# Attention and mixture-of-experts in one kernel: the local maxima's transfer moved two slots ahead and before the keys', the last output projection in two parts, other counts of unread products

## The chip, the cores and the metric

The kernel runs on one core of one Trainium2 chip, as one program. The metric is the device time in microseconds (us) of one execution; lower is better. TensorE is called PE here, VectorE DVE, ScalarE ACT, GpSimd POOL and SyncE SP, as the profile does.

## The reference, cut to what matters

```python
x = L0_attn_x                                   # (16, 512, 256) float32: 8192 tokens of 256
x = x + _layernorm(_L0_attn_ref(_layernorm(x), ...))
x = x + _layernorm(_L0_ffn_ref(_layernorm(x), ...))
...
def _L0_attn_ref(x, ...):
    local_out  = _sliding_window_attn(x @ proj_local,  Wl_in, bl_in, Wl_out, bl_out, 128)
    global_out = _sliding_window_attn(x @ proj_global, Wg_in, bg_in, Wg_out, bg_out, 256)
    w = softmax(fusion_w)
    fused = w[0] * local_out + w[1] * global_out
    return layernorm(fused) * ln_gamma + ln_beta
...
    # in each window, 16 heads of 16:
    scores = q @ k.T / 4 + triu(ones(window, window), k=1)
    o = (softmax(scores) @ v) @ W_out.T + b_out
...
def _L0_ffn_ref(x, w_router, w_gate, w_up, w_down):    # 32 experts, capacity 320
    probs = softmax(xt @ w_router); top1 = argmax(probs); gate = probs[top1]
    slot = top1 * C + position of the token among those of its expert, if that is < C
    y = (silu(buf @ w_gate) * (buf @ w_up)) @ w_down     # per expert, on the slots
    return xt + y[slot] * gate
```

## The kernel before

The 8192 tokens are 32 windows of 256. The attention part is a pipeline of 36 steps, 0 to 35, all written out. In step s five windows are in work: a = s (normalise, transpose, project to queries and keys), b = s - 1 (row scores, from which the row maxima come, and the values' projection), c = s - 2 (scores, exponentials, probabilities times values), d = s - 3 (output projection and layer norms, up to x1, the attention's output with its input added), f = s - 4 (norm before the router, logits, the slot of each token, scatter of the rows to DRAM). Each step has 24 slots, k = 0 to 23. Every engine has its own list, in order; the dictionaries `PE_AT`, `ACT_AT` and `DVE_AT` say in which slot it does what, and `PE_LATE`, `ACT_LATE`, `DVE_LATE` say it for steps 33, 34 and 35. Engines meet through semaphores only.

The first 8 slots have to do with local heads (two heads each), the other 16 with one global head each. In slot k PE makes `scores(k, c)` first (lines 1424 and 1427 local, 1432 and 1434 global), then what the dictionaries put there, and last `row_scores(k, b)` (L1507 local, L1510 global). ACT makes the exponential of `scores(k)`, DVE the maximum over each row of `row_scores(k)` (L1025). `scores(u)` waits for exponential u - 2, `row_scores(u)` for maximum u - 2: there are two PSUM banks for each.

Queries and keys are split into three bf16 parts (high on ACT L774, middle on ACT L780, low on POOL L550) and spread by DMA over 96 partitions of a tile `stack`: six transfers of 128 KB for the local queries, six for the local keys (`spread_local(0)` and `spread_local(1)`, L404), and for the global ones 24 of 64 KB (L413). The maxima of each row, negated and in three parts, are three further rows of `stack`: DVE splits them (`split_l` for the local ones, slots 8 to 11), PE transposes them (`maxima_T`, L1526), ACT copies the result to `mT` (`maxima_out`, L823), and SP moves it to `stack` (`maxima_in`, L425, 24 KB). `scores(0)` of the next step can't start without the local one (`m_in[0]`) and `row_scores(0)` not without the local queries and keys (`spread`).

SP's list in a step, in order: the global maxima's transfer; the second half of the global spread, 12 transfers; the load of `xw` (input of a later window); the store of an output window; the local queries' six, the local keys' six; the load of `xr` (the input again, to be added on POOL L617 to give x1); the local maxima's transfer; the first half of the global spread, 12 transfers. SP waits at each for its own semaphore, so whatever is behind it waits too.

The bank `TR` is used in turn by the global maxima's transposes, the output projection (`op0`, `op1`: for each half q of the window four products over the chunks n of `OnT`, L1605) and the local maxima's transposes. DVE reads the projection and adds the bias to give `fbuf`, called f (L1227). In steps 34 and 35 no scores are left, and the steps are a chain through the norms of window 31, its logits and its scatter. Then the experts run, 16 pairs (L1646, L1659, L1670, L1675), from the scattered rows.

`keep_warm(n)` (L1486) makes n products of 512 columns into a bank that nobody reads. They stand at starts and ends of parts; nine follow the logits in each of steps 34 and 35.

Of the kernel before, what the change touches and what calls it, by code (L numbers as in the profile page):

```python
# [8 lines left out]
def attention_moe_program(nc, T, x, pT_l, pT_g, winT_l, winT_g, woT_l, woT_g, bqk_l, bqk_g, bv_l, bv_g,  # L9
# [4 lines left out]
    P = 128  # L14
# [44 lines left out]
    def num(w):  # L59
        return w[1] if w[0] is None else w[0] * 2 + w[1]  # L60
# [11 lines left out]
    with ExitStack() as ctx:  # L72
# [209 lines left out]


        TR_USES = [("mT_g", 2, mT_ready[1], 1, 0), ("op", 3, f_ready, 1, 0), ("mT_l", 1, mT_ready[0], 1, 0)]
        PE_AT = {"xnT": 0, "p0": 2, "x2T": 3, "mT_g": 4, "p1": 5, "lg": 5, "op0": 7, "op1": 9, "p2": 11, "cs": 14, "mT_l": 15, "p3": 15, "v0": 17, "v1": 20, "g3": 1, "g0": 5, "g1": 12, "g2": 18}
        ACT_AT = {"xnT": 0, "xn2": 1, "p0": 2, "mT_g": 4, "x2T": 4, "mid0": 5, "p1": 5, "o_norm": 5, "mid1": 9, "gate": 10, "p2": 11, "f1": 14, "mid2": 14, "mT_l": 16, "p3": 15, "mid3": 17, "v0": 17, "z": 22, "v1": 20, "norm0": 18}
        DVE_AT = {"split_g": 0, "p0": 3, "fold_g1": 4, "p1": 7, "top": 7, "f": 9, "split_l": 8, "p2": 12, "route": 14, "fold_l0": 10, "p3": 16, "fold_l1": 15, "stats_x": 16, "stats_y": 17, "fold_g0": 22, "stats_x1": 23, "moments_x1": 0, "u3": 1, "u0": 6, "u1": 13, "u2": 18}

        LATE = NW + 1
        PE_LATE = (PE_AT, {**PE_AT, "g3": 1, "x2T": 2, "op0": 3, "op1": 4, "lg": 5, "cs": 14}, {**PE_AT, "g3": 1, "x2T": 2, "op0": 3, "op1": 4, "lg": 5, "cs": 14})  # L290
        ACT_LATE = ({**ACT_AT, "z": 19}, {**ACT_AT, "xn2": 1, "x2T": 2, "o_norm": 3, "f1": 14, "gate": 16, "z": 22}, {**ACT_AT, "xn2": 1, "x2T": 2, "o_norm": 18, "f1": 14, "gate": 16, "z": 22})
        DVE_LATE = ({**DVE_AT, "stats_y": 16, "x1": 21, "stats_x1": 23}, {**DVE_AT, "moments_x1": 0, "u3": 1, "fold_g1": 4, "f": 6, "top": 9, "stats_y": 14, "route": 16, "x1": 21, "stats_x1": 22}, {**DVE_AT, "moments_x1": 0, "u3": 1, "fold_g1": 4, "f": 6, "top": 9, "stats_y": 14, "route": 16, "x1": 21, "stats_x1": 22})

# [85 lines left out]
        def _(sp):  # L379
# [48 lines left out]
            def step(s, par):  # L428
                a, b, c, d, f = stages(s)
                ahead = back(s, -2)  # L430
                if c:
                    maxima_in(1, c, par)
                if b:

                    if d:
                        wait_alone(sp, s2_full, nth(d, UNITS, UNITS - 1))
                    spread_global(0, 1, b, 1 - par)
                    spread_global(1, 1, b, 1 - par)
                if a and (ahead[0] is not None or ahead[1] < NW):

                    wait_alone(sp, xn_ready, nth(a, 1))
                    sp.dma_start(xw[:, par, :, :], x_w[bass.ds(num(ahead), 1)].rearrange("w p q f -> (w p) q f")
                                 ).then_inc(x_in[par], 16)
                if f and num(s) < NW + 3:
                    rows_out(f)
                if a:

                    if c:
                        wait_alone(sp, s2_full, nth(c, UNITS, LU - 1))
                    spread_local(0, a, par)  # L450
                    spread_local(1, a, par)
                if d:

                    if exists(back(d, 2)):
                        wait_alone(sp, x1_ready, nth(back(d, 2), 1))
                    sp.dma_start(xr[:, 1 - par, :, :], x_w[bass.ds(num(d), 1)].rearrange("w p q f -> (w p) q f")
                                 ).then_inc(xr_in[1 - par], 16)
                if b:
                    maxima_in(0, b, 1 - par)
                if a:  # L460

                    if c:
                        wait_alone(sp, s2_full, nth(c, UNITS, UNITS - 9))
                    spread_global(0, 0, a, par)
                    spread_global(1, 0, a, par)
                if s[0] is None and s[1] == NW:
                    for e in range(3):
                        expert_weights(e)
# [913 lines left out]
        def _(pe):  # L1382
# [146 lines left out]
            def step(s, par):  # L1529
# [14 lines left out]
                for k in range(UNITS):  # L1544
# [21 lines left out]
                    if f and k == at["lg"]:  # L1566
                        wait_read(pe, PJ_USES, "lg", s, 2)
                        wait(pe, x2T_ready, f)
                        rows = xn2T[:, :, :].rearrange("p n (q j i) -> p n j q i", q=2, i=32)
                        for n in range(2):  # L1570
                            for j in range(4):
                                last = pe.matmul(pj_bank("lg")[32 * j:32 * j + 32, 0:2 * 32].rearrange("e (q i) -> e q i", q=2), wr[:, n, :], rows[:, n, j, :, :],
                                                 start=(n == 0), stop=(n == 1))
                        last.then_inc(lg_full, 1)
                        if num(s) >= NW + 2:
                            keep_warm(9)
                    if a and k == at["p0"]:
                        wait(pe, xnT_ready, a)
                    for j in range(4):
# [6 lines left out]
                    if f and k == at["cs"]:  # L1586

                        wait_read(pe, PJ_USES, "cs", s, 2)
                        wait(pe, hot_ready, f)
                        bank = pj_bank("cs")  # L1590
                        pe.matmul(bank[:, 0:E], earlier[:, :], hot[:, 0, :], start=True, stop=True)
                        pe.matmul(bank[:, E:2 * E], earlier[:, :], hot[:, 1, :], start=True, stop=False)
                        pe.matmul(bank[:, E:2 * E], onesb[:, :], hot[:, 0, :], start=False, stop=True)
                        pe.matmul(bank[:, 2 * E:3 * E], onesb[:, :], hot[:, 0, :], start=True, stop=False)
                        pe.matmul(bank[:, 2 * E:3 * E], onesb[:, :], hot[:, 1, :], start=False, stop=True).then_inc(cs_full, 1)
                    for q in range(2):
                        if d and k == at[f"op{q}"]:
                            if q == 0:
                                wait_read(pe, TR_USES, "op", s, 1)
                                if s[0] is None and s[1] == 3:  # L1600
                                    pe.wait_ge(const_dve, 2)
                                wait(pe, onT_ready[0], d, 2, 1)
                                wait(pe, onT_ready[1], d, 2, 1)
                            for n in range(4):
                                last = pe.matmul(TR[:, q * D:(q + 1) * D], OnT[:, n // 2, n % 2, q * P:(q + 1) * P], wo[:, n, :],  # L1605
                                                 start=(n == 0), stop=(n == 3))
                            if q == 1:
                                last.then_inc(o_full, 1)
                    if b and k == at["mT_l"]:
                        maxima_T(0, b, s)  # L1610
                    for q in range(2):
                        if b and k == at[f"v{q}"]:
                            project_v(q, b, s, 1 - par)
                    if b:
                        row_scores(k, b, 1 - par)

# [126 lines left out]
```

## Time and profile before

| | |
|---|---|
| Median of 3 runs | 1502.93 us (1502.74 to 1506.17) |
| The profiled execution, its own time | 1501.01 us |
| Its span, first to last instruction | 1499.0 us |
| PE busy | 1431.6 us (96%) |
| DVE busy | 1211.0 us (81%) |
| ACT busy | 889.9 us (59%) |
| POOL busy | 725.7 us (48%) |
| Mean granted clock of PE | 0.991 |

A share of busy time doesn't tell what an engine waits for; the views of waits and of the timeline do. In them a number in brackets is the idle time of that engine just before, and what ended it. The clock is given as a share of full speed: 1.00 is 2.4 GHz and 0.50 is 1.2 GHz. The attention part ends at about 1250 us, the experts' part fills the rest.

### The profile page before, as it was taken

Reading aid. Unit: us, or ns where it says so; the run is one execution under the profiler, and the core shown is the slowest. Engines: PE = TensorE matmul, PEld = TensorE weight load, DVE = VectorE, ACT = ScalarE, POOL = GpSimd, SP = SyncE. Lnnn points to the kernel's source line nnn. Section 1 sums busy time; section 2 is a strip of 40 time slices with the busy share of each in tenths; the row PEclk is TensorE's granted clock in tenths of the full one; section 3 lists DMA queues with packets and bytes.
Section 4 is the critical chain, followed back from the end, with each engine's and each line's share of the span. In section 5 each row is a group of like instructions: output and inputs, shape, how many; then the busy total and the mean of one; then the engine's idle time right before and its main releaser. Section 6 shows DMA issues by size and latency. Waiting matters only on the chain. (4 is left out here: it accounts for less than half of the span.)

```text
span 1499.0 us, 38338 instructions
## 1 busy us (share of the span) xinstructions
PE 1431.6 (96%) x13007; PEld 1047.8 (70%) x13007; DVE 1211.0 (81%) x3509; ACT 889.9 (59%) x1907; POOL 725.7 (48%) x1133
## 2 busy tenths in 40 slices
PE   7789999999999999999999999999999888999995
PEld 4567777777777777777777777777777645777773
DVE  6577888888888888888888888888888763888886
ACT  3356767777777777767776777777676632222220
POOL 4114444544554454544545555555554331566665
PEclk9899999999999999999999999999999999999998
DMA  8997566665677777667777766667666313555641
GB/s 147 166 239 194 118 117 113 111 113 115 118 120 115 114 112 112 110 111 112 116 114 116 111 122 112 115 110 116 109 104 102 103 30 119 157 156 166 190 129 39
DMA packets 253411, 183.32 MB, mean 122 GB/s; under 512 B 29446, under 2 KB 251849, under 8 KB 253216
## 3 DMA queue, kind: packets, MB, share of 16 engines
q1 hardware_dynamic: 232976, 165.14, 59.4%
q10 hardware_dynamic: 13328, 12.00, 3.0%
q0 software_dynamic: 6912, 3.73, 1.1%
q8 instruction: 104, 1.70, 0.6%
q14 instruction: 91, 0.75, 0.2%
HBM read 55.78 MB, written 38.04 MB: 63 GB/s over the span
## 5 line engine op out<-in xcount | busy, mean ns | idle before, releaser
L1025 DVE TENSOR_REDUCE mx<-bank 128x2 f32<-128x512 f32 (+1 forms) x768 | 509.7, 672 | 133.9 <-PE bank L1507 107.8
L763 ACT ACTIVATE pt<-bank 128x512 f32<-128x512 f32 x768 | 438.6, 592 | 145.2 <-PE bank L1434 124.2
L1470 PE MATMUL bank<-xnT,weff 128*128 128x256 f32 x1024 | 248.3, 386 | 1.3 <-ACT xnT L855 0.8
L550 POOL TENSOR_TENSOR parts<-rest,parts 128x512 bf16<-128x512 f32 x128 | 149.5, 1168 | 192.3 <-ACT parts L780 192.3
L1470 PEld LDWEIGHTS bank<-xnT,weff 128*128 128x128 f32 x1024 | 187.7, 191 | 26.8 <-ACT xnT L855 1.0
L1510 PE MATMUL bank<-stack 96*128 96x256 bf16 x1024 | 197.5, 274 | 9.0 <-DVE mx L1025 8.6
L1432 PE MATMUL bank<-stack 128*128 128x256 bf16 x1024 | 195.6, 272 | 2.9 <-DMA stack<-mT 1.5
L1510 PEld LDWEIGHTS bank<-stack 96*128 96x128 bf16 x1024 | 83.7, 97 | 95.6 <-DVE mx L1025 46.7
L774 ACT ACTIVATE parts<-bank,bqk 128x256 bf16<-128x256 f32 x256 | 106.9, 469 | 67.8 <-PE bank L1470 66.2
L1646 PE MATMUL bank<-eT,ew 128*128 128x320 f32 x512 | 143.3, 433 | 0.8 <-ACT eT L897 0.8
L1434 PE MATMUL bank<-tri,identb 128*128 128x226 bf16 x512 | 133.2, 260 | 0.0
L1457 PE MATMUL bank<-pt,v_pad 128*32 128x256 f32 x2048 | 123.8, 382 | 0.8 <-ACT pt L763 0.8
L1605 PE MATMUL bank<-wo,OnT 128*128 128x256 f32 x512 | 122.8, 384 | 1.2 <-DVE OnT L1074 1.2
L1646 PEld LDWEIGHTS bank<-eT,ew 128*128 128x128 f32 x512 | 95.9, 190 | 37.7 <-issue 1.4
L1479 PE MATMUL bank<-weff,xnT 128*128 128x512 f32 x256 | 121.2, 596 | 1.1 <-DVE base L1117 1.1
L526 POOL TENSOR_TENSOR ve<-mv,eps 128x2 f32<-128x2 f32 x128 | 25.9, 202 | 185.0 <-DVE mv L946 184.3
L1424 PE MATMUL bank<-stack 128*128 128x128 bf16 x1024 | 100.3, 220 | 14.3 <-DMA stack<-mT 9.3
L1009 DVE SCALAR_TENSOR_TENSOR rest<-bank,bqk,parts 128x256 f32<-128x256 f32 x256 | 108.6, 465 | 6.4 <-ACT parts L774 6.2
L1432 PEld LDWEIGHTS bank<-stack 128*128 128x128 bf16 x1024 | 94.8, 97 | 20.7 <-ACT pt L763 3.6
L906 ACT ACTIVATE sg<-bank 128x320 f32<-128x320 f32 x64 | 28.0, 437 | 132.6 <-PE bank L1646 132.6
L1605 PEld LDWEIGHTS bank<-wo,OnT 128*128 128x128 f32 x512 | 95.1, 192 | 12.3 <-issue 1.4
L556 POOL TENSOR_TENSOR obuf<-obuf,xrow 128x512 f32<-128x512 f32 x32 | 40.5, 1266 | 130.3 <-ACT obuf L813 130.3
(165 smaller groups left out, 2715.7 us busy)
## 6 DMA issues: line engine op xcount, KB each, us to landing
stack<-parts SPq DMA_DIRECT2D x384, 128.0 KB, 4.9
stack<-parts SPq DMA_DIRECT2D x768, 64.0 KB, 2.6
slots_scratch<-zeros ACTq DMA_DIRECT2D x16, 650.0 KB, 6.3
xr<-x SPq DMA_DIRECT2D x32, 256.0 KB
out<-obuf SPq DMA_DIRECT2D x32, 256.0 KB, 3.2
ew<-w_gate SPq DMA_DIRECT2D x32, 256.0 KB, 3.9
ew<-w_up SPq DMA_DIRECT2D x32, 256.0 KB, 4.8
ew<-w_down SPq DMA_DIRECT2D x32, 256.0 KB, 4.2
```

Source lines behind the costliest of these rows:

```text
L550: pool.tensor_tensor(parts[:, j, 2, :], rest[:, j % 2, :], parts[:, j, 1, :], ALU.subtract).then_inc(lo_ready, 1)
L763: act.activation(pt[:, u % PTR, :], S2[u % 2][:, :], ACT.Exp).then_inc(p_ready, 1)
L1009: last = dve.scalar_tensor_tensor(rest[:, j % 2, cols], pj_bank(f"p{j}")[:, cols], bqk[:, b, 2 * qk + t:2 * qk + t + 1], parts[:, j, 0, co ...
L1025: dve.reduce_max(dst, src, AX.X).then_inc(s1_read, 1)
L1432: pe.matmul(bank[:, kb * WIN:(kb + 1) * WIN], k_stack(par, 1, u - LU, kb * P, P), q_stack(par, 1, u - LU, 0, WIN), start=(kb == 0), stop=F ...
L1434: last = pe.matmul(masked, identb[:, :], tri[:, 0:GLO_COLS].unsqueeze(1).to_broadcast([P, 2, GLO_COLS]), start=False, stop=True)
L1457: last = pe.matmul(PV[32 * h4:32 * h4 + 32, half * WIN:(half + 1) * WIN], v_pad[:, par, kb, 1, 8 * (g - 2) + 4 * half + h4, :], pt[:, (u0 ...
L1470: last = pe.matmul(bank[:, t * WIN:(t + 1) * WIN], weff[:, b, c, qk * D + t * P:qk * D + (t + 1) * P], xnT[:, par, c, :], start=(c == 0), ...
L1479: last = pe.matmul(pj_bank(f"v{q}")[:, :], xnT[:, par, c, q * P:(q + 1) * P], weff[:, :, c, 2 * D:3 * D], start=(c == 0), stop=(c == 1))
L1510: last = pe.matmul(bank[:, n * WIN:(n + 1) * WIN], q_stack(par, 1, u - LU, n * P, P, NPART), k_stack(par, 1, u - LU, 0, WIN, NPART), start ...
L1605: last = pe.matmul(TR[:, q * D:(q + 1) * D], OnT[:, n // 2, n % 2, q * P:(q + 1) * P], wo[:, n, :], start=(n == 0), stop=(n == 3))
L1646: last = pe.matmul(banks[2 + 2 * m + n][:, 0:CAP], ew[:, e % 3, n, c, m * P:(m + 1) * P], eT[:, p % 2, c, e % 2 * CAP:(e % 2 + 1) * CAP], ...
```

## The change

Four things change.

- PE transposes the local maxima in slot 13 instead of 15, ACT copies them in slot 14 instead of 16, and SP issues their transfer between the local queries' six transfers and the local keys' six, instead of behind the keys and the load of `xr`.
- In step 34 the output projection is made in two parts: at slot 1, behind the last product with the values, the chunks 0 to 2 of `OnT` for both halves; at slot 3, once chunk 3 is there, the last chunk for both halves. x2T, the transposes for window 30's logits, goes from slot 2 to slot 4 of PE in that step, so behind it.
- Behind the logits of steps 34 and 35 stand seven unread products instead of nine.
- In step 1 one unread product is put into each of slots 2 to 19, ahead of `row_scores`.

```diff
-        PE_AT = {... "cs": 14, "mT_l": 15, "p3": 15, ...}
-        ACT_AT = {... "mid2": 14, "mT_l": 16, "p3": 15, ...}
+        PE_AT = {... "cs": 14, "mT_l": 13, "p3": 15, ...}
+        ACT_AT = {... "mid2": 14, "mT_l": 14, "p3": 15, ...}
...
-        PE_LATE = (PE_AT, {**PE_AT, "g3": 1, "x2T": 2, "op0": 3, "op1": 4, "lg": 5, "cs": 14}, ...
+        PE_LATE = (PE_AT, {**PE_AT, "g3": 1, "x2T": 4, "op0": 3, "op1": 4, "lg": 5, "cs": 14}, ...
...
                     spread_local(0, a, par)
+                if b:
+                    maxima_in(0, b, 1 - par)
+                if a:
                     spread_local(1, a, par)
                 if d:
...
                     sp.dma_start(xr[:, 1 - par, :, :], x_w[bass.ds(num(d), 1)]...
-                if b:
-                    maxima_in(0, b, 1 - par)
...
                         if num(s) >= NW + 2:
-                            keep_warm(9)
+                            keep_warm(7)
...
+                    if d and num(s) == NW + 2 and k == at["g3"]:
+                        wait_read(pe, TR_USES, "op", s, 1)
+                        wait(pe, onT_ready[0], d, 2, 1)
+                        wait(pe, onT_ready[1], d, 2, 0)
+                        for q in range(2):
+                            for n in range(3):
+                                pe.matmul(TR[:, q * D:(q + 1) * D], OnT[:, n // 2, n % 2, q * P:(q + 1) * P], wo[:, n, :],
+                                          start=(q == 0 and n == 0), stop=False)
+                    if d and num(s) == NW + 2 and k == at["op0"]:
+                        wait(pe, onT_ready[1], d, 2, 1)
+                        for q in range(2):
+                            last = pe.matmul(TR[:, q * D:(q + 1) * D], OnT[:, 1, 1, q * P:(q + 1) * P], wo[:, 3, :], start=False, stop=(q == 1))
+                        last.then_inc(o_full, 1)
                     for q in range(2):
-                        if d and k == at[f"op{q}"]:
+                        if d and num(s) < NW + 2 and k == at[f"op{q}"]:
...
+                    if num(s) == 1 and 2 <= k < 20:
+                        keep_warm(1)
                     if b:
                         row_scores(k, b, 1 - par)
```

NW is 32, so NW + 2 is step 34.

## Rows read from the trace of the kernel before

**Rows 1.** PE's waits over the span; then the page's group of line 1605

```profile
PE bank L1424 <- DMA stack<-mT: 9.3, 11, 3.3
...
L1605 PE MATMUL bank<-wo,OnT 128*128 128x256 f32 x512 | 122.8, 384 | 1.2 <-DVE OnT L1074 1.2
```

**Rows 2.** PE's timeline: four step starts (start us, us, engine, line, operation)

```profile
427.12 0.60 PE L1557 MATMUL bank<-ident,xn 128*128 128x128 f32 x4
...
721.22 0.60 PE L1557 MATMUL bank<-ident,xn 128*128 128x128 f32 x4
...
757.06 0.60 PE L1557 MATMUL bank<-ident,xn 128*128 128x128 f32 x4
...
974.07 0.60 PE L1557 MATMUL bank<-ident,xn 128*128 128x128 f32 x4
```

**Rows 3.** PE's timeline at one of the longer steps' ends

```profile
646.86 0.40 PE L1424 MATMUL bank<-stack 128*128 128x128 bf16 x4 [1.48 <-DMA stack<-mT]
```

**Rows 4.** SP's timeline in the step before it

```profile
630.36 7.70 SPq L404 DMA_DIRECT2D stack<-parts  x12
...
638.79 0.77 SPq L425 DMA_DIRECT2D stack<-mT  x1
```

**Rows 5.** Windows there: engines' busy us, PE's clock, DMA share, GB/s

```profile
633.80:643.80 10.00, 10.00 (x79) 5.96 (x78) 9.20 (x30) 7.55 (x16) 6.62 (x12) 1.00 1.17 134
643.80:645.80 2.00, 1.58 (x14) 0.79 (x11) 2.00 (x5) 2.00 (x5) 1.70 (x2) 1.00 1.12 191
```

**Rows 6.** ACT's timeline: `f1` in that step and in the step from 757.06

```profile
633.46 1.08 ACT L793 ACTIVATE fbuf<-fbuf,mr,rstd 128x256 f32<-128x256 f32 x2
...
781.07 1.08 ACT L793 ACTIVATE fbuf<-fbuf,mr,rstd 128x256 f32<-128x256 f32 x2
```

**Rows 7.** SP's timeline in the step from 757.06

```profile
775.94 8.37 SPq L404 DMA_DIRECT2D stack<-parts  x12
```

**Rows 8.** Windows in that step: the last two columns are DMA share and GB/s

```profile
779.10:789.10 10.00, 10.00 (x91) 6.80 (x88) 9.77 (x31) 7.22 (x15) 5.18 (x9) 1.00 1.16 132
789.10:791.10 2.00, 2.00 (x9) 0.93 (x8) 1.57 (x4) 1.91 (x5) 1.44 (x4) 1.00 1.17 194
```

**Rows 9.** Timelines of DVE and PE behind the step end of rows 3

```profile
649.53 0.75 DVE L938 BATCH_NORM_STATS2 bst<-xrow 128x6 f32<-128x256 f32 x2 [3.07 <-POOL xrow L617]
...
653.62 0.63 PE L1551 MATMUL bank<-ident,xn 128*128 128x128 f32 x4 [0.22 <-ACT xn L799]
```

**Rows 10.** Timelines of PE and ACT around the start of step 2

```profile
62.59 0.59 PE L1424 MATMUL bank<-stack 128*128 128x128 bf16 x4 [3.28 <-DMA stack<-mT]
...
66.51 2.55 PE L1470 MATMUL bank<-xnT,weff 128*128 128x256 f32 x8
...
64.50 0.59 ACT L855 ACTIVATE xnT<-bank 128x512 f32<-128x512 f32 x1
```

**Rows 11.** PE's waits in 30 to 60 us; the window behind, with PE's clock

```profile
PE bank L1510 <- DVE mx L1025: 4.6, 8, 1.0
...
61.00:67.80 6.80, 5.21 (x31) 4.62 (x32) 1.57 (x4) 2.28 (x4) 0.00 (x0) 0.50 1.18 147
```

**Rows 12.** PE's timeline in step 34

```profile
1216.42 0.63 PE L1551 MATMUL bank<-ident,xn 128*128 128x128 f32 x4 [0.92 <-DVE xn L1169]
1218.28 5.30 PE L1605 MATMUL bank<-wo,OnT 128*128 128x256 f32 x16 [1.22 <-DVE OnT L1074]
...
1223.87 2.12 PE L1486 MATMUL bank<-tri,identb 128*128 128x512 bf16 x9
```

**Rows 13.** Timelines of POOL and DVE in step 34

```profile
1221.78 1.27 POOL L556 TENSOR_TENSOR obuf<-obuf,xrow 128x512 f32<-128x512 f32 x1 [1.07 <-ACT obuf L813]
...
1223.62 0.69 DVE L1227 TENSOR_TENSOR fbuf<-bank,bias_row 128x512 f32<-128x512 f32 x1 [5.49 <-PE bank L1605]
...
1225.75 0.70 POOL L530 TENSOR_TENSOR rstd<-ve,mhalf 128x2 f32<-128x2 f32 x1
...
1227.88 0.88 DVE L1143 SCALAR_TENSOR_TENSOR ybuf<-ybuf,rstd,beta_row 128x256 f32<-128x256 f32 x2
```

More of the change, by code:

```diff
@@ L284, in attention_moe_program @@
         TR_USES = [("mT_g", 2, mT_ready[1], 1, 0), ("op", 3, f_ready, 1, 0), ("mT_l", 1, mT_ready[0], 1, 0)]
-        PE_AT = {"xnT": 0, "p0": 2, "x2T": 3, "mT_g": 4, "p1": 5, "lg": 5, "op0": 7, "op1": 9, "p2": 11, "cs": 14, "mT_l": 15, "p3": 15, "v0": 17, "v1": 20, "g3": 1, "g0": 5, "g1": 12, "g2": 18}
-        ACT_AT = {"xnT": 0, "xn2": 1, "p0": 2, "mT_g": 4, "x2T": 4, "mid0": 5, "p1": 5, "o_norm": 5, "mid1": 9, "gate": 10, "p2": 11, "f1": 14, "mid2": 14, "mT_l": 16, "p3": 15, "mid3": 17, "v0": 17, "z": 22, "v1": 20, "norm0": 18}
+        PE_AT = {"xnT": 0, "p0": 2, "x2T": 3, "mT_g": 4, "p1": 5, "lg": 5, "op0": 7, "op1": 9, "p2": 11, "cs": 14, "mT_l": 13, "p3": 15, "v0": 17, "v1": 20, "g3": 1, "g0": 5, "g1": 12, "g2": 18}
+        ACT_AT = {"xnT": 0, "xn2": 1, "p0": 2, "mT_g": 4, "x2T": 4, "mid0": 5, "p1": 5, "o_norm": 5, "mid1": 9, "gate": 10, "p2": 11, "f1": 14, "mid2": 14, "mT_l": 14, "p3": 15, "mid3": 17, "v0": 17, "z": 22, "v1": 20, "norm0": 18}
         DVE_AT = {"split_g": 0, "p0": 3, "fold_g1": 4, "p1": 7, "top": 7, "f": 9, "split_l": 8, "p2": 12, "route": 14, "fold_l0": 10, "p3": 16, "fold_l1": 15, "stats_x": 16, "stats_y": 17, "fold_g0": 22, "stats_x1": 23, "moments_x1": 0, "u3": 1, "u0": 6, "u1": 13, "u2": 18}
         LATE = NW + 1
-        PE_LATE = (PE_AT, {**PE_AT, "g3": 1, "x2T": 2, "op0": 3, "op1": 4, "lg": 5, "cs": 14}, {**PE_AT, "g3": 1, "x2T": 2, "op0": 3, "op1": 4, "lg": 5, "cs": 14})
+        PE_LATE = (PE_AT, {**PE_AT, "g3": 1, "x2T": 4, "op0": 3, "op1": 4, "lg": 5, "cs": 14}, {**PE_AT, "g3": 1, "x2T": 2, "op0": 3, "op1": 4, "lg": 5, "cs": 14})
         ACT_LATE = ({**ACT_AT, "z": 19}, {**ACT_AT, "xn2": 1, "x2T": 2, "o_norm": 3, "f1": 14, "gate": 16, "z": 22}, {**ACT_AT, "xn2": 1, "x2T": 2, "o_norm": 18, "f1": 14, "gate": 16, "z": 22})
```

## The prediction

> **What bounds the kernel now.** I read the page first. TensorE (PE) is busy 96% of the span; it sets the pace, so a part of the change is worth what it takes from PE's waits, or from the chain where PE only waits. The table of PE's waits comes next [rows 1]: its longest entry is the transfer of the maxima (`stack<-mT`), 9.3 us in 11 waits. Third, PE's timeline around step starts; I date a step by the transposes of line 1557. An undisturbed stretch of six steps takes 974.07 - 757.06 = 217.01 us, 36.17 each; the eight steps from 427.12 to 721.22 take 294.10 [rows 2]. Against 8 x 36.17 = 289.36 these lose 4.7 us. In [rows 3] the reader sees how: PE has nothing left before `scores(0)`, line 1424, and sits for 1.48 us until the transfer lands. Fourth, SyncE's queue (SP) shows why: the transfer of 24 KB is issued at 638.79 and is there at 646.86, 8 us later, since it stands behind twelve of 128 KB and `xr` [rows 4]. The DMA engines are full meanwhile (share 1.17 and 1.12): 134 GB/s in the middle of it, with 191 in 643.8 to 645.8 [rows 5], says that the twelve (1.57 MB, 11.8 us at 134) are through at about 644.7, and the first six at 638.8.
>
> **The local transfer, two slots sooner and ahead of the keys.** PE's two transposes move from slot 15 to 13: same work. They can't add a wait: `row_scores(13)` in the same slot waits for VectorE's (DVE) maximum(11), and that stands behind the last split on DVE's list. The copy on ScalarE (ACT), counted 0.4 us, moves behind the two activations of `f1`, which end at 634.54 [rows 6]; it pushes exp(15) back by that much, and PE asks for that only two slots on. So mT is ready at about 634.9. SP reaches it at 634.2 at the soonest (630.36 plus half of 7.70 [rows 4]) and waits 0.7; it issues mT (0.77), then the six key transfers from about 635.8 instead of 634.2, then `xr`, then the global ones. So the keys are issued 1.7 us later here. In the regular step that starts at 757.06, `f1` ends at 782.15, mT is ready at 782.5, and the keys are issued in 783.3 to 787.2, where the twelve were done at 784.31: 2.9 us later [rows 6, 7]. Queued behind SP's waiting instruction are: the six keys (for `row_scores(0)` of the next step), `xr` (for x1 on GpSimd, POOL), and twelve global ones, first needed in slot 8 of the next step. What hides the later issue is the queue's backlog: the six query transfers still keep the engines busy until about 638.8, and the keys' first come before that. I take it that the keys land 0.3 to 1 us later only. In the regular step they are there by 791.1, when the stage of 132 to 194 GB/s ends [rows 8], and PE wants them at 757.06 + 36.17 + 0.4 = 793.6; in the step that ends at 646.86 it would want them at 646.4 and has them at 644.7 plus up to 1.
>
> The Trainium skill, "DMA: Bandwidth & Descriptors", section "Rules for kernel authors", speaks against this order: a transfer whose slowest dimension is below 16 keeps to that many DMA engines. The destination of mT has three rows, so its 48 pieces of 512 B would pile on three engines, now ahead of the keys. No row here tells engines apart; by that rule the keys would come at the late end of my range, and the sum would be about 1 us smaller. The numbers below don't need it.
>
> Worth: with mT early, all steps would take 36.17. That is 4.7 us in the eight steps. Of the table's 9.3 us, 3.3 stand at 62.59 [rows 10]; 6.0 - 4.7 = 1.3 are left elsewhere, of which I take 0.6, half: **5.3 us**. But `xr` gives some back. Where it lands late, POOL's x1 is late, then its statistics, and then x2T in slot 3. At 649.53 they start 2.27 us after PE's step start (646.86 + 0.40), and PE waits 0.22 [rows 9]; so each us beyond 2.05 costs one. With the stall of 1.48 gone the step starts about 1.3 sooner, and the wait becomes 1.5. Two weaker cases of the kind I put at half of that together, 0.8: 2.3 us, which lessens the 5.3. **Steady part: 3.0 us**; bounds 0 and 6.0.
>
> **Unread products in step 1, and its end.** 18 products of 512 columns are put in (slots 2 to 19). Nine of line 1486 take 2.12 us at the upper clock [rows 12], 0.213 each between starts: 3.8 us of PE work. Their cover: step 1 has eight waits of 4.6 us for DVE in its global half alone [rows 11], and then the stall of 3.28 us. If the cover were gone, they would cost 3.8. In that stall sits the gain. Without it PE still can't run on: ACT makes exp(0) and xnT only behind its list of weight DMAs, xnT at 64.50 to 65.09, and p0 can't start before 65.15; it started at 66.51 [rows 10]: 1.35. Also p0's eight instructions took 2.55 us, where eight of that shape take 1.9 at 0.24 each [rows 1], in a stretch with the clock granted at 0.50, its lower level of 1.2 GHz, after the stall [rows 10, 11]; with a shorter one I count 0.45 back. **1.8 us**. Bounds: 3.8 lost, or the whole stall, 3.3, gained.
>
> **The last output projection.** In step 34 only the chain counts. PE ends `values` at about 1215.5 (1216.42 less the idle 0.92), waits 1.22 for OnT until 1218.28, and then makes all 16 instructions (8 products of two each) in 5.30 us; DVE's f starts at 1223.62 [rows 12, 13]. Now 12 of 16 run from 1215.5: at 0.24 each (122.8 us for 512 [rows 1]) that is 2.9 us, to 1218.4, and 4 behind the wait take 0.95: f at about 1219.3, 4.3 us sooner. What is late next? POOL: it has the residual until 1223.05 and only then makes rstd for f: 0.3 for two small ones and 0.70, so 1224.1, against 1226.45. DVE's second scaling, at 1227.88, needs it [rows 13]: 1224.2. So **3.7 us**. x2T, moved behind the four products, starts at 1219.3 instead of 1216.42, and its logits come at about 1221.1, when DVE has just finished f's statistics. That move costs nothing while f's chain is the longer; if the logits were the last, they would eat up to 0.5. Two fewer unread products after the logits give at most 2 x 0.213 = 0.4 in each of the last two steps, if DVE's `hot` isn't later; I count 0.1. **Sum 3.8**; bounds 2.9 (the clock stays at the lower level, so four products and x2T take twice as long) and 4.7. The experts' part hides none of it, since it starts on the last scatter.
>
> **Sum.** 3.0 + 1.8 + 3.8 = 8.6 us. The profiled execution took 1501.01 (span 1499.0), so 1492.4 for it. The median of the runs is 1.9 above it, 1502.93: **1494.3 us**.
>
> **Rivals.** (1) *The keys land as late as they are issued*: the queue runs dry between queries and keys. Regular steps: 791.1 + 2.9 = 794.0 against 793.6, 0.4 in each of 22; in the eight others 645.8 + 1.7 = 647.5 against 646.4, 1.1 each: 17.6 of new stalls, for 5.3 of old ones. 1494.3 + 3.0 + 12.3 = 1509.6, slower. For it: in the regular step the twelve end near 790.4, so the first six near 784.5, and the keys' issue now starts at 783.3, little ahead. Against: ahead is ahead, and only a dry queue makes it so. It decides once (8.6 + 4.5) / 30 = 0.4 us are lost per step. Chance 0.07. (2) *Only the eight slow steps stall*: 8 x 1.1 = 8.8 in place of 5.3; 1494.3 + 3.0 + 3.5 = 1500.8, no change. Chance 0.10. (3) *The products in step 1 lie on the path* and the start gains nothing: 1494.3 + 1.8 + 3.8 = 1499.9, no change. Against: the cover above. Chance 0.05. My forecast has 0.78.
>
> **Range.** Highest gain 6.0 + 3.3 + 4.7 = 14.0: 1488.9. Upwards cases (2) and (3) begin at 1499.9; I take 1489 to 1500. A difference under 0.3% (4.5 us) can't be told from no change with this kernel. Faster 0.78, same 0.15, slower 0.07.
>
> **What the profile after would show.** Waits for `stack<-mT` at `scores(0)` gone or one or two; no or few waits of `row_scores` for `stack<-parts`; in SP's list the transfer from mT between two groups of six; x2T waiting 1 to 2 us in some steps with a late `xr`; the clock around 61 to 67.8 less low; in step 34 twelve instructions before and four behind the wait for OnT, f about 4.3 sooner, and the start of the experts about 8.6 sooner. Wrong would make it: keys that wait in every step, or an experts' part that lasts longer.

## The result, and the profile after

The changed kernel takes 1497.87 us (median of 7 runs, 1494.49 to 1500.03) against 1502.93 us (7 runs, 1500.07 to 1506.17) for the kernel before: ratio 0.9962, 95% interval [0.9947, 0.9976]. That is 5.1 us or 0.3% faster: inside the range, 3.6 us above the 1494.3 forecast, and about 0.6 of the 8.6 us that were to be gained.

The profiled execution took 1497.85 us, its span is 1496.0: 3.0 us less than before. (The profile before was 1.9 us faster than the median of its kernel, this one lies on the median.) PE's waits over the span and its busy time on the page (engine, line, what it waited for, us in total, times, longest):

```profile
PE 1433.1 (96%) x13021; PEld 1047.0 (70%) x13021; DVE 1214.9 (81%) x3509; ACT 874.9 (58%) x1907; POOL 722.8 (48%) x1133
...
PE bank L1425 <- ACT pt L764: 7.5, 30, 2.1
...
PE bank L1511 <- DVE mx L1026: 7.0, 12, 2.3
PE bank L1508 <- issue: 5.0, 2, 2.7
PE bank L1552 <- ACT xn L800: 4.7, 7, 1.5
```

The entry `stack<-mT`, 9.3 us [rows 1], is gone. In its place L1508 (`row_scores` of local heads; lines have moved by one) has two waits of 5.0 us in all with no releaser named; by the code it waits there for the local queries and keys or for DVE's maximum, and in step 4 DVE's last maximum had ended 2.4 us before PE went on. So I read them as waits for keys. L1552 (x2T) has 4.7 us in 7. To see where the 3.0 us came from I cut both executions at step starts, PE's transposes of xn. Before:

```profile
29.95 0.38 PE L1557 MATMUL bank<-ident,xn 128*128 128x128 f32 x2
...
173.58 0.38 PE L1557 MATMUL bank<-ident,xn 128*128 128x128 f32 x2
...
1118.97 0.38 PE L1557 MATMUL bank<-ident,xn 128*128 128x128 f32 x2
...
1249.96 0.88 PE L1631 MATMUL bank<-ident,zb 128*128 128x128 f32 x6
```

After, with the wait in step 4 among them, and the experts' start:

```profile
30.84 0.60 PE L1558 MATMUL bank<-ident,xn 128*128 128x128 f32 x4
...
137.34 0.60 PE L1558 MATMUL bank<-ident,xn 128*128 128x128 f32 x4
140.62 0.38 PE L1508 MATMUL bank<-stack 96*128 96x128 bf16 x4 [2.67 <-issue]
...
177.58 0.38 PE L1558 MATMUL bank<-ident,xn 128*128 128x128 f32 x2
...
1119.67 0.38 PE L1558 MATMUL bank<-ident,xn 128*128 128x128 f32 x2
...
1246.98 0.88 PE L1647 MATMUL bank<-ident,zb 128*128 128x128 f32 x6
```

| stretch | before | after | gain |
|---|---|---|---|
| to the start of step 1 | 29.95 | 30.84 | -0.9 |
| steps 1 to 4 | 143.63 | 146.74 | -3.1 |
| steps 5 to 30 | 945.39 | 942.09 | +3.3 |
| step 31 to the experts | 130.99 | 127.31 | +3.7 |
| experts | 249.0 | 249.0 | 0 |

So the middle and the end came as forecast (3.0 and 3.8), and the start went the other way. Three things more are needed for what follows. First, in the middle nothing waits for keys, and x2T waits for ACT 2.1 us in all, as was forecast; PE's waits in 180 to 1120 us:

```profile
PE bank L1425 <- ACT pt L764: 4.0, 25, 0.2
PE bank L1552 <- ACT xn L800: 2.1, 5, 0.7
```

SP's list in a regular step (from 757.69) has the new order; the keys are issued until 788.16, 3.2 us later from the step's start than in [rows 7]:

```profile
777.48 3.83 SPq L404 DMA_DIRECT2D stack<-parts  x6
783.44 0.78 SPq L425 DMA_DIRECT2D stack<-mT  x1
784.32 3.84 SPq L404 DMA_DIRECT2D stack<-parts  x6
788.26 0.55 SPq L459 DMA_DIRECT2D xr<-x  x1
```

Second, step 3. The same part of SP's list, and the windows there (last three columns: PE's clock, DMA share, GB/s):

```profile
123.24 7.15 SPq L404 DMA_DIRECT2D stack<-parts  x6
130.49 0.77 SPq L425 DMA_DIRECT2D stack<-mT  x1
131.39 5.44 SPq L404 DMA_DIRECT2D stack<-parts  x6
```

```profile
128.00:132.00 4.00, 4.00 (x42) 1.91 (x40) 3.51 (x10) 2.94 (x6) 3.21 (x6) 1.00 0.98 241
132.00:136.00 4.00, 4.00 (x28) 2.54 (x24) 3.09 (x9) 2.92 (x6) 2.11 (x7) 1.00 0.49 115
136.00:140.00 4.00, 1.94 (x18) 1.19 (x16) 2.17 (x5) 3.24 (x7) 0.00 (x0) 1.00 1.13 134
140.00:144.00 4.00, 3.38 (x33) 1.69 (x37) 0.83 (x3) 0.60 (x1) 2.17 (x2) 0.64 0.97 158
```

Six query transfers take SP 7.15 us to issue here, not 3.83, and the keys 5.44. SP is done with the keys at 136.83, only 1.1 us before PE wants them (137.34 + 0.6); in the step from 757.69 it is 6.2 us. PE waits 2.67 us, its clock is lower behind the wait (0.64 in the last window), and step 4 lasts 40.24 us (137.34 to 177.58) where a regular one lasts 36.1. From 132 to 136 the DMA engines also work at 0.49 only: the queue runs dry, as in the first rival. Whether that makes the wait, the experiments have to tell.

Third, step 34, against [rows 12, 13]: PE, DVE and POOL:

```profile
1215.98 2.86 PE L1603 MATMUL bank<-wo,OnT 128*128 128x256 f32 x12
1218.74 1.13 PE L1608 MATMUL bank<-wo,OnT 128*128 128x256 f32 x4
1219.91 0.69 DVE L1228 TENSOR_TENSOR fbuf<-bank,bias_row 128x512 f32<-128x512 f32 x1 [1.22 <-PE bank L1608]
1222.34 1.26 POOL L557 TENSOR_TENSOR obuf<-obuf,xrow 128x512 f32<-128x512 f32 x1 [1.07 <-ACT obuf L814]
1222.72 0.91 DVE L1098 CAST idx_f<-top_i 128x2 f32<-128x2 uint32 x1
1223.86 0.70 POOL L531 TENSOR_TENSOR rstd<-ve,mhalf 128x2 f32<-128x2 f32 x1
1224.97 0.88 DVE L1144 SCALAR_TENSOR_TENSOR ybuf<-ybuf,rstd,beta_row 128x256 f32<-128x256 f32 x2
```

Twelve instructions before the wait and four behind it. The products with the values begin 0.55 us later here than before (1214.12 against 1213.57), so f, at 1219.91, is 1223.62 + 0.55 - 1219.91 = 4.3 us sooner, and the second scaling 1227.88 + 0.55 - 1224.97 = 3.5.

Part of these 4.3 us is the clock. The 16 products took 5.30 us before and take 2.86 + 1.13 = 3.99 us now. Before, PE's granted clock was 0.69 over them, of which the lower level from about 1218.1 to 1221.6, behind two waits; now it is 1.00:

```profile
1218.28:1223.58 5.30, 5.30 (x20) 4.16 (x24) 0.00 (x0) 0.91 (x2) 3.47 (x6) 0.69 0.02 3
...
1215.98:1219.91 3.93, 3.93 (x22) 3.22 (x19) 2.48 (x6) 0.00 (x0) 2.46 (x5) 1.00 0.02 4
```

So about 3.0 us come from the twelve instructions moved ahead of the wait, and 1.3 from the spell of the lower clock that stays away.

### The profile page after: what moved, and what is told of

It is laid out like the page before. It is cut to its first block and busy times, and to the rows that moved or that the text cites. A ratio compares the mean times of both kernels' runs of the same rounds, so it can differ in the third digit from the quotient of the medians.

```text
span 1496.0 us, 38366 instructions
## 1 busy us (share of the span) xinstructions
PE 1433.1 (96%) x13021; PEld 1047.0 (70%) x13021; DVE 1214.9 (81%) x3509; ACT 874.9 (58%) x1907; POOL 722.8 (48%) x1133
## 5 line engine op out<-in xcount | busy, mean ns | idle before, releaser
L1511 PEld LDWEIGHTS bank<-stack 96*128 96x128 bf16 x1024 | 85.3, 97 | 94.2 <-issue 47.8
L1662 PE MATMUL bank<-eT,ew 128*128 128x320 f32 x512 | 143.3, 433 | 0.8 <-ACT eT L898 0.8
L1662 PEld LDWEIGHTS bank<-eT,ew 128*128 128x128 f32 x512 | 96.2, 191 | 37.4 <-issue 1.4
L1619 PE MATMUL bank<-wo,OnT 128*128 128x256 f32 x496 | 117.5, 380 | 0.0
L1508 PE MATMUL bank<-stack 96*128 96x128 bf16 x1024 | 100.1, 220 | 5.9 <-issue 5.0
L1508 PEld LDWEIGHTS bank<-stack 96*128 96x128 bf16 x1024 | 73.5, 97 | 40.4 <-issue 19.6
## 6 DMA issues: line engine op xcount, KB each, us to landing
stack<-parts SPq DMA_DIRECT2D x384, 128.0 KB, 4.6
```

Source lines behind the costliest of these rows:

```text
L1508: last = pe.matmul(bank[:, (2 * n + j) * P:(2 * n + j + 1) * P], q_stack(par, 0, 2 * u + n, j * P, P, NPART), k_stack(par, 0, 2 * u + n, j ...
L1511: last = pe.matmul(bank[:, n * WIN:(n + 1) * WIN], q_stack(par, 1, u - LU, n * P, P, NPART), k_stack(par, 1, u - LU, 0, WIN, NPART), start ...
L1662: last = pe.matmul(banks[2 + 2 * m + n][:, 0:CAP], ew[:, e % 3, n, c, m * P:(m + 1) * P], eT[:, p % 2, c, e % 2 * CAP:(e % 2 + 1) * CAP], ...
```

## The experiments

Times are medians; a ratio is to the kernel before on the same chip. The kernel before spread over 14 us in one set of 35 runs (1498.76 to 1513.04) and over 7 and 12 us in the two others, the versions over 4 to 10 us, so I lean on the stretches of the profiles, cut as above. Each is one execution, so differences of a stretch that are smaller than those between two profiles of one kernel show nothing.

| version | steps 1 to 4 | steps 5 to 30 | 31 to experts | ratio, interval |
|---|---|---|---|---|
| before | 143.6 | 945.4 | 131.0 | |
| before, second profile | 150.9 | 948.0 | 131.1 | |
| changed | 146.7 | 942.1 | 127.3 | 0.9962 [0.9947, 0.9976] |
| changed, second profile | 146.0 | 941.4 | 127.6 | |
| transfer alone | 146.7 | 941.9 | 131.0 | 0.9968 [0.9947, 0.9988] |
| products alone | 144.8 | 943.6 | 132.9 | 0.9991 [0.9972, 1.0009] |
| projection alone | 148.0 | 946.7 | 129.3 | 0.9978 [0.9961, 0.9995] |
| changed, SP's list as before | 147.3 | 942.8 | 128.0 | 0.9961 [0.9943, 0.9978] |
| changed, new order from step 4 | 143.3 | 941.6 | 127.8 | 0.9950 [0.9933, 0.9968] |
| changed, `xr` first | 147.0 | 939.2 | 127.5 | 0.9945 [0.9927, 0.9963] |
| both of these | 143.2 | 938.8 | 127.4 | 0.9930 [0.9904, 0.9957] |
| changed, zero fills spread | 143.6 | 943.1 | 127.5 | 0.9955 [0.9937, 0.9973] |
| changed, old slots | 146.8 | 963.2 | 130.8 | 1.0129 [1.0093, 1.0165] |
| changed, x2T in slot 2 | 145.8 | 940.2 | 128.0 | |

### One part at a time

The transfer alone: the slots of PE and ACT and the order on SP, on the kernel before.

```diff
-"mT_l": 15   # PE_AT
+"mT_l": 13
-"mT_l": 16   # ACT_AT
+"mT_l": 14
...
                     spread_local(0, a, par)
+                if b:
+                    maxima_in(0, b, 1 - par)
+                if a:
                     spread_local(1, a, par)
```

> Only the local maxima's transfer is changed: slots 13 and 14, and ahead of the keys in SP's list. Theory A: this part gains about 3.3 us in steps 5 to 30 and loses about 4 us where row_scores(0) of step 4 waits for the keys (a wait of 2 to 3 us at about 140 us, the DMA share low just before it, then a stretch at the half clock). In sum it stands within 1.5 us of before, and step 4 lasts about 40 us. Theory B: the wait in step 4 has to do with the products put into step 1. Then this kernel has no such wait, step 4 lasts 36 us, and it is 3 to 4 us faster than before.

Measured: 1500.03 us against 1504.97. Steps 5 to 30 take 941.9 us; step 4 lasts 40.0 us and has the wait, 2.5 us, without any product in step 1. Theory A holds for the place of the wait. Its price came out smaller against the runs (ratio 0.9968) than against the first profile, for a reason that the next profiles show.

The products alone:

```diff
+                    if num(s) == 1 and 2 <= k < 20:
+                        keep_warm(1)
                     if b:
                         row_scores(k, b, 1 - par)
```

> Only the 18 unread products in step 1. Theory A: they cost nothing that lasts and gain little, since the end of step 1 waits for transfers: within 1 us of before, the stall of some 3 us at scores(0) of step 2 still there, step 4 lasts 36 us. Theory B: step 4 lasts about 40 us here too, and the kernel is 3 to 4 us slower than before.

Measured: 1503.31 us, ratio 0.9991: no difference that can be told. The stall at `scores(0)` of step 2 is still there, 3.35 us. Step 4 lasts 35.8 us, so theory B falls. The last stretch, 132.9 us in the table, holds a spell of the lower clock at 1176 to 1188 us (0.82 and 0.89 in windows of 6 us), which the kernel before doesn't have there.

The projection alone, with nine products behind the logits:

```diff
+                    if d and num(s) == NW + 2 and k == at["g3"]:
+                        ...  # chunks 0 to 2 of both halves
+                    if d and num(s) == NW + 2 and k == at["op0"]:
+                        ...  # chunk 3 of both halves
-"x2T": 2   # PE_LATE, step 34
+"x2T": 4
```

> Only the last output projection in two parts, with x2T moved behind it in step 34; nine unread products stay. The prediction's step: 3.7 us faster, f on DVE 4.3 us sooner after the end of the values' products, y's second scaling 3.7 us sooner. Rival: the scatter of window 30, or the output's rows on POOL, hold the end, and it gains 1 to 2 us.

Measured: 1500.91 us, ratio 0.9978, which is 3.3 us [0.8, 5.9]. Counted from the start of the last products with the values, f comes 4.3 us sooner and the second scaling 3.5, as in the changed kernel. The stretch from step 31 shows 129.3 instead of 131.0, but that profile has a spell of the lower clock level at 1186 us. The eight other profiles with the projection split and the new slots have none there, and in them the stretch takes 127.3 to 128.0: 3.0 to 3.8 us less than 131.0 and 131.1, the two profiles of the kernel before, and than 131.0, the transfer alone, which has the new slots and the old projection.

The changed kernel with SP's list as before:

```diff
                     spread_local(0, a, par)
-                if b:
-                    maxima_in(0, b, 1 - par)
-                if a:
                     spread_local(1, a, par)
...
+                if b:
+                    maxima_in(0, b, 1 - par)
```

> The changed kernel with SP's list as before: PE's and ACT's slots for the local maxima stay at 13 and 14, but the transfer is again issued behind the keys and the load of xr. Theory A (the place in SP's list makes both the gain in the middle and the loss in step 4): step 4 lasts 36 us again, but the stalls at scores(0) in the middle are back (about 4 to 6 us), so within 1 us of the changed kernel. Theory B: step 4 stays at 40 us, and the kernel is 3 us or more slower than the changed one.

Measured: 1499.12 us, ratio 0.9961. Neither theory as written. Step 4 lasts 37.4 us, but step 3 now ends with 3.5 us at `scores(0)`, and steps 1 to 4 take 147.3. In the middle some stalls for the maxima are back:

```profile
PE bank L1424 <- DMA stack<-mT: 2.8, 4, 1.0
PE bank L1424 <- issue: 2.8, 9, 0.8
```

and yet steps 5 to 30 take 942.8, nearly as little as with the new order. So the earlier slots by themselves seem to be worth most of the middle's gain; it is one profile against 943.6 to 948.0 in the four with the old slots and order. Part of it is that an undisturbed step lasts 36.12 instead of 36.17 us; why, no run here tells.

### Is the start steady?

Both kernels once more, unchanged.

> The kernel before, unchanged, for one more profile. If the start of the kernel is steady, steps 1 to 5 take 143.6 us again and the stall at scores(0) of step 2 is 3.3 us. If it varies by itself, they take up to 148 us, as the same stretch did with only the projection changed (147.95).

Measured: 1511.66 us for this execution. Steps 1 to 4 take 150.9 us, 7.2 more than in the first profile of the same program, with a wait of 3.4 us at the end of step 3 that the first had as 0.9. PE's waits in the first 180 us:

```profile
PE bank L1424 <- DMA stack<-mT: 6.4, 2, 3.4
```

So the first profile had caught a good start. Versions with the old order took 143.6, 150.9, 144.8, 148.0 and 147.3 us in steps 1 to 4, 146.9 in the mean; those with the new order in all steps and the fills as before 146.7, 146.0, 146.7, 147.0, 146.8 and 145.8, 146.5 in the mean. The change moves the start by less than the start moves by itself.

> The changed kernel, unchanged, for one more profile. If the wait for the keys in step 4 belongs to the order of the transfers, it is there again, at 2 to 3 us, and step 4 lasts about 40 us; if it was a chance of the one execution, it is gone.

Measured: 1497.15 us; the wait for the keys in step 4 is there, 1.7 us, and step 4 lasts 38.4 us, both less than expected. It is there in all five profiles with the new slots, the new order in every step and the fills as before (the changed kernel twice, the transfer alone, `xr` first, x2T in slot 2), with 1.7 to 2.7 us. It is no chance.

### The wait for the keys in step 4

The new order only from step 4 on:

```diff
-                if b:
+                if b and num(s) >= 4:
                     maxima_in(0, b, 1 - par)
...
+                if b and num(s) < 4:
+                    maxima_in(0, b, 1 - par)
```

> The changed kernel, but in steps 1 to 3 the local maxima's transfer stands behind the keys and the load of xr in SP's list, as before; from step 4 on it stands ahead of the keys. Theory A (in step 3 the queue runs dry between queries and keys, so the keys' landing follows their later issue): the wait of 2.7 us at row_scores(0) at the start of step 4 is gone or under 1 us, step 4 lasts 36 to 37.5 us, steps 5 to 30 take 942 us as in the changed kernel; from step 1 to step 5 it takes about 144 us instead of 146.7. Rival: the start of the kernel varies by some us by itself, in any version, and the wait only takes another name (scores(0) for the maxima): steps 1 to 5 take 146 to 148 us again, and the time is within 1 us of the changed kernel.

Measured: 1497.12 us, ratio 0.9950. Step 4 lasts 35.8 us, no wait for keys, 1.6 us for the maxima in its place, at the end of step 3; steps 1 to 4 take 143.3. These are theory A's numbers, but they don't rule its rival out. Up to the end of step 3 this kernel issues its transfers exactly like the version with SP's list as before, and that one waited 3.5 us there and took 147.3. In the seven profiles with the old order in step 3 the wait for the maxima is 0.9 to 3.5 us, 2.0 in the mean, and steps 3 and 4 together take 72.0 to 76.1, 73.4 in the mean. In the five with the new order the wait for the keys is 2.2 us in the mean and the two steps take 73.0 to 75.5, 74.3 in the mean. So the wait takes another name, as the rival says, and the new order costs the start some 0.8 us, less than it varies by itself.

The zero fills, 16 transfers of 650 KB which ACT issues in steps 2 and 3, spread as 6, 4 and 6 over steps 2 to 4:

```diff
-if s[1] in (2, 3) and k < 16 and k % 2 == 1:
-    zero_slots((s[1] - 2) * 8 + k // 2)
+if s[1] in (2, 3, 4) and k % 2 == 1 and k < (12, 8, 12)[s[1] - 2]:
+    zero_slots((0, 6, 10)[s[1] - 2] + k // 2)
```

> The changed kernel with the 16 zero fills of the slots (650 KB each, from ACT's queue) spread over steps 2 to 4 as 6, 4, 6 instead of 8 and 8 in steps 2 and 3. Theory: SP issues slowly in step 3 (0.9 us for a key transfer instead of 0.64) and the queue runs dry because the fills crowd the DMA engines; with half of them in step 3 the query and key transfers are issued faster and the wait for the keys at row_scores(0) of step 4 goes from 1.8 to 2.7 us to under 1 us. Rival: SP is late for another reason, and the wait stays at 2 us or more; then steps 1 to 5 take 146 us or more.

Measured: 1496.58 us, ratio 0.9955. SP's list in step 3:

```profile
121.95 4.00 SPq L404 DMA_DIRECT2D stack<-parts  x6
128.45 0.77 SPq L425 DMA_DIRECT2D stack<-mT  x1
129.34 4.18 SPq L404 DMA_DIRECT2D stack<-parts  x6
```

The order is the same as in the changed kernel, but six transfers take SP 4.0 and 4.2 us, the keys start 2 us sooner, the wait is gone, and step 4 lasts 36.1 us. In the changed kernel the last fill is issued at 124.8 us, beside the queries; here the last one of step 3 at 115.0. The wait moved in part: step 5, behind the fills of step 4, now lasts 38.0, with 0.90 us at `row_scores(0)` and 0.95 at x2T. So the fills make the keys late.

But a dry queue is not what makes the wait. Either is seen without the other: with the fills spread the DMA share is 0.53 from 128 to 132, and 0.10 in the us from 129, and PE doesn't wait; in the transfer alone it is never below 1.08 from 128 to 138, and PE waits 2.49 us.

```profile
128.00:132.00 4.00, 4.00 (x29) 2.25 (x30) 3.32 (x9) 3.98 (x10) 3.66 (x3) 1.00 0.53 100
```

```profile
132.00:136.00 4.00, 4.00 (x26) 2.47 (x25) 3.35 (x9) 3.45 (x7) 1.72 (x6) 1.00 1.13 154
```

What goes with the wait is how long before PE's demand SP is done with the keys: 1.1 to 3.8 us in the five profiles with the wait, 5.8 with the fills spread, 6.2 in the regular step (and 5.0 in the later one behind the spread fills, with its 0.90 us). How long the keys take to land behind that isn't the same in all: the wait ends 5.2 and 5.9 us after the end of their issue in the transfer alone and in `xr` first, 3.4 to 3.8 us in the other three. So SP's late issue and full DMA engines can both have a part; the runs don't tell them apart.

### How much cover is left in the middle

The old slots 15 and 16 with the new order, so that SP waits longer with the keys behind it:

```diff
-"mT_l": 13   # PE_AT
+"mT_l": 15
-"mT_l": 14   # ACT_AT
+"mT_l": 16
```

> The changed kernel, but PE and ACT make the local maxima's transposes and copy in slots 15 and 16 as before, while SP's list keeps the transfer ahead of the keys. SP then waits some 1.5 us longer, with the keys behind it. Theory (the backlog of the query transfers covers the later issue, up to a point which the changed kernel has nearly reached): the queue now runs dry, the keys land 1 us or more later, and row_scores(0) waits for them in most steps, 0.3 to 1 us each; steps 5 to 30 take 950 to 965 us. Rival: the queue has more cover than that, and they stay at 942.

Measured: 1522.96 us, ratio 1.0129: 19 us slower than before, 24 than the changed kernel by the span. Steps 5 to 30 take 963.2, as the theory said, but by a longer way. SP's list and PE's waits (180 to 1140 us):

```profile
384.21 3.87 SPq L404 DMA_DIRECT2D stack<-parts  x6
391.94 0.77 SPq L425 DMA_DIRECT2D stack<-mT  x1
392.81 3.84 SPq L404 DMA_DIRECT2D stack<-parts  x6
```

```profile
PE bank L1552 <- ACT xn L800: 13.6, 25, 1.3
PE bank L1508 <- issue: 2.9, 6, 0.9
```

SP stands still for 3.9 us (388.08 to 391.94) and then has the keys and `xr` behind it. The keys account for 2.9 us; x2T, late through `xr`, x1 and its statistics, for 13.6, in nearly every step. That is why the most regular steps last 36.62 us here, half a us more.

### The load of xr, and the best version

`xr` at the head of SP's list in each step:

```diff
+                if d:
+                    if exists(back(d, 2)):
+                        wait_alone(sp, x1_ready, nth(back(d, 2), 1))
+                    sp.dma_start(xr[:, 1 - par, :, :], ...)
                 if c:
                     maxima_in(1, c, par)
...
                     spread_local(1, a, par)
-                if d:
-                    ...
```

> The changed kernel with the load of xr moved to the head of SP's list in each step, where the DMA engines are nearly idle. Theory: the waits of x2T for ACT, 2.1 us in 5 between 180 and 1120 us, come from xr landing late, so they go, the keys land about 1 us sooner, and steps 5 to 30 take 939 to 940 us instead of 942.1. Rival: the late statistics have another cause (z on ACT), and the waits stay: 942.

Measured: 1495.65 us, ratio 0.9945. No wait of x2T between 180 and 1120 us is left, steps 5 to 30 take 939.2:

```profile
PE bank L1425 <- ACT pt L764: 2.6, 16, 0.2
PE bank L1425 <- issue: 1.3, 8, 0.2
PE bank L1508 <- issue: 0.7, 1, 0.7
```

Both edits together, the new order from step 4 and `xr` first:

> The changed kernel with both: the load of xr at the head of SP's list, and the local maxima's transfer ahead of the keys only from step 4 on. If the two effects add, steps 1 to 5 take 143 to 145 us, steps 5 to 30 take 939.2, the part from step 31 to the experts 127.5, and it is 4 to 5 us faster than the changed kernel, about 10 us faster than before. Rival: the start varies by itself by as much, so steps 1 to 5 take 146 to 148 here and it is only 2.5 us faster than the changed kernel.

Measured: 1493.72 us, ratio 0.9930 [0.9904, 0.9957]: 10.5 us faster than before by the ratio, 8.7 by the medians. The middle is that of `xr` first, 938.8, which is 26 steps of 36.11. The start, 143.2, is as short as with the new order from step 4 alone, but by what is said there it may owe that to chance. PE's only waits in the middle:

```profile
PE bank L1427 <- ACT pt L766: 3.7, 23, 0.2
```

### The place of x2T in step 34

```diff
-"x2T": 4   # PE_LATE, step 34
+"x2T": 2
```

> The changed kernel with x2T left in slot 2 in step 34, between the two parts of the last projection. The prediction's reading (POOL's rstd, not PE, holds y's second scaling): f comes 0.3 to 0.7 us later than in the changed kernel, but the part from step 31 to the experts stays at 127.3 to 127.8 us. Rival: f's chain is the bound, and the part takes 0.5 us more, 128 or above.

One profile: the stretch takes 128.0 us, the rival's side of the line, against 127.3 and 127.6. Counted from the start of the last products with the values, f comes 0.3 us later and the second scaling 0.5. This profile has a spell of the lower clock from about 1223 us, but the second scaling starts at 1222.63, so its half us is not the clock's. POOL's rstd was ready at 1221.78; DVE's list held the scaling, in which one small instruction had lost 1.0 us (last section). Whether the chain of f or that loss sets the end stays open.

## Why the prediction was right or wrong

**Steady part, forecast 3.0 us: right.** 3.3 in the pair of profiles. The four profiles with the middle as before take 943.6 to 948.0, 945.9 in the mean, the five with the middle of the changed kernel 940.2 to 942.1, 941.4 in the mean: 4.5 us less (the one with the fills spread, whose step 5 waits behind fills, left out). The stalls at `scores(0)` are gone. The give-back by `xr` was forecast as 2.3; x2T waits 2.1 us (0.2 before), and the version with `xr` first, without these waits, gains 2.9 in the middle, which shows that it hangs on `xr`. The keys, forecast 0.3 to 1 us later, make no wait in 26 steps. Not foreseen: the slots alone shorten the undisturbed step by 0.05 us and seem to bring most of the gain; the new order adds about 1 us net of what `xr` costs, by one profile.

**The last projection, 3.8: right.** 3.7 in the pair, f 4.3 us sooner as worked out. The sum took the 16 instructions at the upper clock's 0.24 us without saying that the 5.30 us before held a spell of the lower level; 1.3 of the 4.3 us hang on that spell staying away. The lower bound of 2.9 was for that case. The reading of what comes next was wrong: I had POOL's rstd hold the second scaling. It was ready at 1224.56, but DVE began at 1224.97, since its own list had lost 0.74 us on one instruction (below). So 3.5 instead of 3.7 there; that the two products fewer gave the rest isn't shown.

**The end of step 1 and the products, forecast 1.8: wrong.** Nothing of it is left: steps 1 and 2 take 71.24 us against 71.67 before, 71.61 with the transfer alone and 71.47 with the products alone. The stall at `scores(0)` is gone, but two others stand in its place, and behind them p0 is slow:

```profile
62.23 0.38 PE L1508 MATMUL bank<-stack 96*128 96x128 bf16 x4 [2.33 <-issue]
65.82 0.61 PE L1425 MATMUL bank<-stack 128*128 128x128 bf16 x4 [2.10 <-ACT pt L764]
66.55 3.31 PE L1471 MATMUL bank<-xnT,weff 128*128 128x256 f32 x8
```

Counted from the start of step 1, p0 starts 0.85 us sooner (35.71 instead of 36.56), where 1.35 was forecast; and its eight instructions take 3.31 us, not 2.55, where 0.45 was to come back. The step that failed is that a shorter stall gives the upper clock back: the idle time was only shared out, 4.4 us in two pieces for 3.3 in one, and the keys' wait was not in the sum. The products are neither cost nor gain that can be measured.

**The keys in the start: wrong.** "I take it that the keys land 0.3 to 1 us later only" was drawn from steps 17 and 21 and applied to all. In step 3 SP needs 7.15 us for six transfers where I reckoned 3.85, the fills being in flight, and is done with the keys 1.1 us before PE wants them: 2.67 us of wait and a spell at the lower clock level behind it, 4.1 us in that step. The version with the fills spread has no such wait. The first rival, the dry queue, is seen in that profile, but not in all that wait, so it is not the cause. Against the profile before this looks like a loss of 3.1 us in steps 1 to 4; over all profiles it is some 0.8, since with the old order the start waits for the maxima instead.

**The base, and the sum.** I had made the sum against a profile whose steps 1 to 4 were 1.1 to 7.2 us shorter than in the four others with the old order in every step. A single profile can't tell that; the second one did. It accounts for the ratio of the runs, 5.7 us [3.6, 8.0], being more than the 3.0 of the pair of spans. Over all profiles the three parts are 4.5, -0.8 and 3.0 to 3.8 us, where 3.0, 1.8 and 3.8 were forecast: the middle gave more, for reasons that I hadn't seen, and that made up for about half of what the start lacked. That much of the agreement is luck.

**The rule of the Trainium skill** ("DMA: Bandwidth & Descriptors", "Rules for kernel authors") on transfers with few rows in their slowest dimension: the keys came late enough in no regular step to see it, so these runs neither bear it out nor contradict it.

## What to carry to other kernels

A transfer moved ahead in a queue is paid for by those behind it. Whether they notice has to be looked up in each stage, above all where other transfers run beside them: take the time from the end of their issue to where they are wanted. The DMA share alone misleads. When a stall is taken away, look at what else was just in time: here `xr`, whose early issue was worth nearly as much again (2.9 us) as the change's middle part (3.3). When a chain has idle time in it, read the clock behind it too: 1.3 of the 4.3 us by which f came sooner were the clock's. And profile the kernel before twice before weighing effects of a few us.

## What the runs showed of the hardware that was not expected

- While POOL makes its addition of 128x512 (1222.34 to 1223.60), DVE's cast of 128x2 takes 0.91 us and ends at 1223.63; the same cast takes 0.16 to 0.18 us in the other 31 steps. In the version with x2T in slot 2, DVE's tensor_scalar of 128x2 takes 1.19 us and ends within 0.03 us of the end of the same addition:

```profile
1219.50 1.26 POOL L557 TENSOR_TENSOR obuf<-obuf,xrow 128x512 f32<-128x512 f32 x1 [1.07 <-ACT obuf L814]
...
1219.60 1.19 DVE L1092 TENSOR_SCALAR ntop<-top 128x2 f32<-128x2 f32 x1
```

  DVE's small operation is held until POOL's is over. The Trainium skill, "SBUF — State Buffer", section "Who interferes with whom", says that casts and tensor_scalar of DVE in its two-port modes and any operation of POOL take one shared pair of ports as an exclusive lock, and that the one that comes second stands still; this trace agrees, with 1223.63 against 1223.60 us. Which mode the cast ran in no row shows.

- The like is seen in nearly every step, with an instruction of two inputs: DVE's TENSOR_TENSOR of 128x64 (`posh<-pos,hot`) takes 0.20 to 0.22 us where it meets no large operation of POOL, and 0.96 or 0.97 us in the 28 steps where it begins inside POOL's TENSOR_TENSOR of 128x512 (L596, 1.27 us).

- SP's issue of one transfer of 128 KB takes 0.64 us in a regular step (six in 3.83 us), though the DMA share is 1.16 there, at 132 GB/s [rows 8]. In step 3, with ACT's fills of 650 KB beside it and 241 to 304 GB/s from 120 to 132 us, the six for the queries take 6.3 to 7.7 us in the five profiles with the new order, 1.1 to 1.3 each; with the fills spread they take 4.0.
- The same program, on the same data, has starts that differ by 7 us (143.6 and 150.9 us for steps 1 to 4), while steps 5 to 30 of the best version keep 36.10 to 36.11 us each.
